# Gate roots moved to GpSimd in eight pieces, third norm's statistics derived from the second's, VectorE side work placed behind the row minimum

## The chip, the cores and the metric

One core of a Trainium2 chip runs the whole program in one launch. The metric is the device time of that core in microseconds (us), the median of several executions; a lower time is better. The engines are TensorE (PE; PEld is its weight load), VectorE (DVE), ScalarE (ACT), GpSimd (POOL) and SyncE (SP, which here only issues DMAs).

## The reference, cut to what matters

The input is 16 sequences of 1024 tokens with 128 features. Each goes through an embedding with six gated convolutions, then a two-map attention, then a feed-forward part with expert weights:

```python
h = tok(x)                                  # embedding, 6 gated convolutions
h = h + attn(layernorm(h))
h = h + ffn(layernorm(h))

# attn, 8 heads of 16 features, L = 1024, windows of 4 rows:
attn1 = softmax(q1 k1 / 4); attn2 = softmax(q2 k2 / 4)
# per window and map: mean, std, max, min of the attention rows
std = jnp.std(r, axis=-1, ddof=1).mean(axis=-1)
alpha = sigmoid(relu(relu(gate_in @ gw1 + gb1) @ gw2 + gb2) @ gw3 + gb3)
out = (alpha * attn1 + (1 - alpha) * attn2) @ v @ Wo

# ffn: normalises its input again
mu = xf.mean(-1); var = xf.var(-1)
normed = (xf - mu) / sqrt(var + 1e-5) * ln_g + ln_b
x_attn = normed @ attn_w.T + attn_b + xf
y = fc2(gelu(fc1(x_attn))); out = gelu(y @ next_w.T + next_b)
```

The ffn normalises what the layernorm before it has already normalised: these are the second and the third norm below. The standard deviation per attention row is a square root of a variance; there are 16 units (2 maps x 8 heads) x 8 row tiles = 128 such columns of 128 rows for a sequence.

## The kernel before, in words

Work on a sequence ("batch") is a fixed pipeline of 128 steps, 16 units j of 8 steps n each; 16 batches follow one another in a loop, with a prologue ahead and a tail behind. In every step

- PE makes a tile of scores (`ps_s`, line 389 by the helper `mm`), adds a tile to the weighted sum (`ps_o`), makes a tile of transposed scores (`ps_t`), and then does the step's side tasks (`ps_w`);
- DVE copies and negates the scores with their maximum (`row_max`, L715, `neg_s`), does the step's side tasks, and then takes the row minimum of the tile before (`row_min`, L723);
- ACT takes the exponential of the transposed scores (`exp_t`, L586), does its side tasks, and then takes the sum of squares of the softmax rows (`squares`, L579, `junk`).

The score buffers are two deep (`ps_s`), so PE can be about two steps ahead of DVE; `ps_t` is single, so PE and ACT alternate on it. Every engine takes its instructions in order.

Side tasks are everything else of the network: the convolutions of the next batch (`conva`, `convg`), projections, the gate and the feed-forward part of the batch before. `plan()` writes them once, before the program is built, into a list for each step (`STEP[n]`); it uses a cost for PE (`COST`), one for POOL (`POOL_COST`, `STEP_WEIGHT`), gaps in steps between tasks (`GAP`), and allowed places within a unit (`SLOTS`). All engines go through the same list in the same order, so a task that waits holds up what stands behind it on its engine.

The tasks that the change touches or that stand near it:

- `snap` (step 16): DVE takes the reciprocal of the softmax sums (L762), POOL then makes the gate's features in `gin` and the two attention outputs (L943 to L959). The variances are left in `gtmp[:, 3, :]`.
- `std` (step 21): two ACT square roots (L610) write the feature columns of `gin`. `win` (step 23) multiplies `gin` on PE, DVE copies the result to `winm` (L764). `hid1`, `hid2`, `logit`, `alpha` follow.
- `msplit` j (two steps ahead of `mrow` j): POOL splits the 8 row maxima of the unit before into three bf16 parts (L866, L914, L916); `mrow` j (first step of unit j) transposes them on DVE (L755), and SP then issues four DMAs of them (L337) and the 12 loads of the next unit (L330). PE needs the rows four steps later.
- `unit` j: DVE takes up a finished unit's output (L731) and POOL two small statistics (L879). For j = 2 DVE waits for POOL's `snap`.
- `convg`: POOL closes a piece of a convolution with four instructions.
- `ln1`, `ln2`, `ln3`: DVE takes mean and variance (`moments`, L735 and L739), POOL normalises (`normalise`, L866, L885, L886, L888). L885 is the power with exponent -0.5 on a 128x8 tile. `ln3` (step 48) is the third norm; it reads `ln2`'s result.

In units 0 and 15 the tasks `qk` (four POOL instructions each) stand ahead of `msplit` 1 and `msplit` 15.

In the tail, after the loop, the same post-processing runs once for the last batch, one task after another, with nothing beside it.

Of the kernel before, what the change touches and what calls it, by code (L numbers as in the profile page):

```python
# [24 lines left out]
P = 128  # L25
L = 1024
# [27 lines left out]
def two(kind):  # L54
    return [(kind, 0), (kind, 1)]
# [5 lines left out]
POST = ([("snap",), ("std",), ("win",), ("hid1",), ("hid2",), ("logit",), ("alpha",)] + two("attT") + two("wo")  # L61
# [5 lines left out]
    "std": ("act",),  # L67
    "win": ("pe", "dve"), "hid1": ("pe", "dve"), "hid2": ("pe", "dve"), "logit": ("pe", "act", "pool"),
    "alpha": ("pe", "dve", "pool"), "attT": ("pe", "act"), "wo": ("pe", "dve"), "ln2": ("dve", "pool"),
    "ln3": ("dve", "pool"), "nT": ("pe", "act"), "attw": ("pe", "act"), "fc1": ("pe", "act"), "gelu1": ("act",),  # L70
# [11 lines left out]
             "ln1": 66, "ln2": 66, "ln3": 66, "gelu2": 24, "vcopy": 15}  # L82
# [3 lines left out]
GAP = {("std",): 5, ("win",): 2, ("hid1",): 2, ("hid2",): 2, ("logit",): 2, ("alpha",): 2, ("attT", 0): 4,  # L86
# [12 lines left out]
def plan():  # L99

    at = {n: [] for n in range(STEPS)}
    for j in range(U):
        at[j * T].append(("mrow", j))
        at[j * T + LAG_V % T - 1].append(("unit", j))
    for n, task in {0: ("gather",), 2: ("vcopy", 0), 3: QK[1][0], 5: QK[1][1], 8: QK[1][2], 10: QK[1][3],
                    14: ("vcopy", 1)}.items():
# [4 lines left out]
    share = cost(BODY_TASKS) / (STEPS - 2 * T)
    behind = 0
    for n in range(STEPS):
        behind = max(behind - STEP_WEIGHT, 0) + sum(POOL_COST.get(t[0], 0) for t in at[n])
        for stage in (post, pre):
            tasks, first = stage
            while tasks and first <= n and n % T in SLOTS.get(tasks[0][0], range(T)):
                task = tasks[0]
                done = cost([t for m in range(n) for t in at[m]])
                on_pe = task[0] in COST  # L120
                if on_pe and (cost(at[n]) or stage is pre and done + COST[task[0]] / 2 > share * (n + 1)):
                    break
                if task[0] in ("conva", "convg") and behind > STEP_WEIGHT:
                    break
                if stage is pre and any(t[0] in ("gelu1", "gelu2", "std") for t in at[n]):
                    break
                at[n].append(tasks.pop(0))
                behind += POOL_COST.get(task[0], 0)
                if task == ("wo", 1):
                    at[n].append(("hcopy",))  # L130
                first = n + (GAP.get(tasks[0], SPREAD.get(tasks[0][0], 1)) if tasks else 0)
            stage[1] = first
    assert not post[0] and not pre[0], (post, pre)
    for j in range(1, U + 1):
# [27 lines left out]
def tower_kernel(nc, ids, table, consts, w_e2h, b_e2h, conv_w, conv_b, w_h2e, b_h2e, wq1, wk1, wq2, wk2, wv, wo,  # L162
# [4 lines left out]
    with ExitStack() as ctx:  # L167
        def sb(name, shape, dt=F32):
            return ctx.enter_context(nc.sbuf_tensor(name, shape, dt))
# [28 lines left out]
        rs_pow = sb("rs_pow", [P, T])  # L198

# [187 lines left out]
        def _(pe):  # L387
# [53 lines left out]
            def task(phase, i, tk):  # L441
# [6 lines left out]
                if kind == "win":  # L448
                    w("act", ("std",))
# [120 lines left out]
        def _(act):  # L570
# [24 lines left out]
            def task(phase, i, tk):  # L595
# [11 lines left out]
                elif kind == "std":  # L607
                    w("pool", ("snap",))
                    for a in range(2):
                        last = nc.scalar.activation(  # L610
                            gin[:, :, :, 4 * a + 1].rearrange("p t h -> p h t"),
                            gtmp[:, 3, U * T // 2 * a:U * T // 2 * (a + 1)].rearrange("p (h t) -> p h t", h=H),
                            ACT.Sqrt)
# [84 lines left out]
        def _(dve):  # L698
# [43 lines left out]
            def task(phase, i, tk):  # L742
# [77 lines left out]
            nc.vector.memset(rs_pow[:, :], -0.5)  # L820
            nc.vector.memset(xc[:, :, 0:1], 0.0)
# [12 lines left out]
            pos.update(loop=True, base=pos["n"], n=0, per=3)  # L834
# [17 lines left out]
        def _(pool):  # L852
# [37 lines left out]
            def task(phase, i, tk):  # L890
# [37 lines left out]
                elif kind == "snap":  # L928
# [22 lines left out]
                    ts(gtmp[:, 3, :], gtmp[:, 1, :], 1.0 / (L - 1), 0.0, ALU.mult, ALU.max)  # L951
# [7 lines left out]
                    last = feature(3, lambda dst, a: tt(dst, of2(0, a), of(recip, a), ALU.mult))  # L959
                elif kind == "logit":  # L960
# [58 lines left out]
            for tk in BODY:  # L1019
                per += {"msplit": 3, "snap": 5, "alpha": 1, "ln2": 3, "ln3": 3, "convg": 3, "ln1": 3, "qk": 3}.get(tk[0], 0)  # L1020
# [62 lines left out]
```

How the kernel before makes its waits and increments, by code:

```python
        def wait_side(eng, phase, i, of, task=None):  # L272
            eng.wait_ge(side_sem[of], side.upto(phase, i, of, task))
# [41 lines left out]
        @block.sync  # L316
# [35 lines left out]
                sp.dma_start(out[i], z[:, :, :]).then_inc(s_out, 16)  # L352
            load_ids(0)
            for dst, src in weight_loads:
                sp.dma_start(dst, src).then_inc(s_load, 16)
            wait_side(sp, "pre", 0, "pool", QK[0][-1])
            load_unit(0)
            with sp.Fori(0, NB // E) as group:
                for e in range(E):
                    i = group * E + e
                    sp.wait_ge(s_emb, i * (16 * T) + 16 * T)
                    settle()
                    load_ids(i + 1)
                    load_expert("body", i, e)
                    for j in range(U):
                        if j:
                            sp.wait_ge(s_st, i * STEPS + T * (j - 3) + T + LAG_T)
                        else:
                            sp.wait_ge(s_exp, i * STEPS + 1)
                        settle()
# [5 lines left out]
                        if ("gelu2",) in sum((STEP[n] for n in range(j * T, j * T + T)), []):  # L378
                            store_out("body", i)
            load_expert("tail", NB, 0)
            store_mrow("tail", NB, 0)
            store_out("tail", NB)
            sp.wait_ge(s_out, 16 * (NB + 2))
# [57 lines left out]
            def task(phase, i, tk):  # L441
# [48 lines left out]
                    _, c, j = tk  # L490
                    if (c, j) == (0, 0):
                        pe.wait_ge(s_exw, i * 64 + 64)
                    w("act", ("attw", c))
```

## Time and profile before

| | us |
|---|---|
| median of 3 runs (5943.18 to 5953.85) | 5952.06 |
| the profiled execution | 5952.66 |
| its span | 5950.7 |
| its granted TensorE clock, mean | 0.947 |

| stretch of the span | us |
|---|---|
| prologue | 0 to 137.5 |
| 2048 steps in 16 batches | 137.5 to 5827.8 |
| tail | 5827.8 to 5950.7 |

The span is that of the instructions; 2 us lie around it. A batch takes 5690.3 / 16 = 355.6 us, a step 2.78 us on average. The sixth batch (1914.4 to 2268.0 us) stands for all: its stretches, and single instructions of it, are read below. A step n of it starts where DVE's L715 starts: step 16 at 1954.1, step 21 at 1966.8, step 24 at 1977.3, step 36 at 2009.1, step 50 at 2051.0, step 80 at 2128.1, step 104 at 2204.8.

### The profile page before, as it was taken

What the parts mean: (1) busy time and instruction counts of PE and PEld (TensorE: products, weight loads), DVE (VectorE), ACT (ScalarE), POOL (GpSimd) and SP (SyncE); (2) the same over time, 40 slices, a digit from 0 to 9 for tenths busy, and PEclk for the clock granted to TensorE, in tenths of its full rate; (3) what the DMA queues carried; (4) which work ended last, traced back from release to release, by engine and by line L of the source; (5) the groups of instructions that cost most, each with busy time, mean ns of one, the idle gap of its engine ahead of it and who ended that gap; (6) DMA issues with size and microseconds to landing.
All of it is one profiled execution on the core that took longest, in us unless ns stands there. A gap on an engine that the chain in (4) does not pass through costs nothing.

```text
span 5950.7 us, 121038 instructions
## 1 busy us (share of the span) xinstructions
PE 5237.1 (88%) x34070; PEld 2513.5 (42%) x34070; DVE 5105.1 (86%) x7715; ACT 5201.0 (87%) x7937; POOL 2445.9 (41%) x4439
## 2 busy tenths in 40 slices
PE   6988989899898988989889898988989899898985
PEld 4443434444343443434344343443435344343443
DVE  2989899898998989899888988989899898989982
ACT  2998989889898999989889898998989889898893
POOL 6525344252433525344352434425353352534422
PEclk8999999999999999999999999999999999999996
DMA  1011010011101001010010101001010110101010
GB/s 38 19 23 27 18 31 20 21 27 24 27 20 29 20 21 27 20 31 19 22 28 22 27 20 28 20 23 27 22 27 20 24 24 21 27 20 30 18 23 10
DMA packets 164934, 140.87 MB, mean 24 GB/s; under 512 B 89197, under 2 KB 108269, under 8 KB 164141
## 3 DMA queue, kind: packets, MB, share of 16 engines
q1 hardware_dynamic: 159100, 124.09, 9.1%
q0 software_dynamic: 4352, 8.92, 0.7%
q8 instruction: 291, 4.77, 0.4%
q14 instruction: 375, 3.06, 0.2%
q10 hardware_dynamic: 816, 0.02, 0.0%
HBM read 21.26 MB, written 8.91 MB: 5 GB/s over the span
## 4 chain that ended last, share of the span: by engine, by line
PE 43%; ACT 24%; issue 15%; DVE 8%; POOL 6%; SPq 1%; ACTq 1%; DMA 1%; POOLq 0%; DVEq 0%
PE ps_w L389 19%; PE ps_t L389 10%; ACT junk L579 10%; ACT exps L586 8%; PE ps_o L389 8%; PE ps_s L389 6%; DVE neg_s L715 4%; DVE rowmin L723 2%; ACT hpre L590 2%; SPq L330 1%; DVE bn L735 1%; POOL part L866 1%; POOL ctmp L998 1%; POOL part L1000 1%; ACT L579 1%
## 5 line engine op out<-in xcount | busy, mean ns | idle before, releaser
L715 DVE TENSOR_SCALAR_CACHE_REDUCE neg_s<-ps_s 128x1024 f32<-128x1024 f32 x2048 | 2492.3, 1217 | 464.2 <-PE ps_s L389 399.0
L579 ACT ACTIVATE junk<-neg_s,negmax 128x1024 bf16<-128x1024 f32 x2048 | 2358.8, 1152 | 227.6 <-DVE neg_s L715 222.6
L723 DVE TENSOR_REDUCE rowmin<-neg_s 128x1 f32<-128x1024 f32 x2049 | 2467.3, 1204 | 0.0
L586 ACT ACTIVATE exps<-ps_t 128x1024 f32<-128x1024 f32 x2060 | 2112.6, 1026 | 171.2 <-PE ps_t L389 166.5
L389 PE MATMUL ps_t<-qst,kst 99*128 99x512 bf16 x4120 | 1300.6, 399 | 441.3 <-ACT exps L586 436.9
L389 PE MATMUL ps_o<-exps,v_cur 128*32 128x256 f32 x16512 | 1365.3, 404 | 133.2 <-DVE o_raw L731 112.2
L389 PE MATMUL ps_s<-kst,qst 96*128 96x512 bf16 x4096 | 1272.0, 392 | 65.3 <-DMA kst<-part 49.2
L389 PE MATMUL ps_w<-xc,cw 128*128 128x256 f32 x4704 | 1199.3, 392 | 1.0
L389 PEld LDWEIGHTS ps_w<-xc,cw 128*128 128x128 f32 x4704 | 922.4, 197 | 229.8 <-ACT chan L590 8.9
L866 POOL TENSOR_SCALAR ctmp<-ug 128x256 f32<-128x256 f32 x408 | 164.7, 404 | 1593.3 <-ACT ug L655 1577.9
L389 PEld LDWEIGHTS ps_t<-qst,kst 99*128 99x128 bf16 x4120 | 237.3, 98 | 1369.3 <-ACT exps L586 771.3
L389 PEld LDWEIGHTS ps_o<-exps,v_cur 128*32 128x32 f32 x16512 | 330.6, 109 | 1061.8 <-issue 691.3
L389 PEld LDWEIGHTS ps_s<-kst,qst 96*128 96x128 bf16 x4096 | 397.4, 101 | 494.5 <-issue 158.9
L579 ACT ACTIVATION_READ_ACCUMULATOR junk<-neg_s,negmax 128x1 f32 x2048 | 412.1, 201 | 0.0
L986 POOL TENSOR_TENSOR ctmp<-ctmp,va 128x256 f32<-128x256 f32 x408 | 297.3, 729 | 34.1
L987 POOL TENSOR_TENSOR ctmp<-ctmp,xc 128x256 f32<-128x256 f32 x408 | 278.5, 683 | 32.0
L866 POOL TENSOR_SCALAR mparts<-negmax 128x8 bf16<-128x8 f32 x256 | 51.8, 202 | 564.8 <-DVE neg_s L715 524.3
L590 ACT ACTIVATE va<-ps_w,cb 128x256 f32<-128x256 f32 x392 | 185.2, 472 | 80.6 <-PE ps_w L389 68.3
L655 ACT ACTIVATE ug<-ps_w,cb_half 128x256 f32<-128x256 f32 x392 | 186.5, 476 | 75.5 <-PE ps_w L389 74.7
L866 POOL TENSOR_SCALAR xc<-ctmp 128x256 f32<-128x256 f32 x408 | 166.5, 408 | 67.7 <-POOL ctmp L987 67.7
L866 POOL TENSOR_SCALAR part<-stage 128x512 bf16<-128x512 f32 x132 | 81.8, 619 | 259.8 <-ACT stage L590 241.2
L715 DVE DVE_READ_ACCUMULATOR neg_s<-ps_s 128x1 f32 x2048 | 168.4, 82 | 0.0
(181 smaller groups left out, 4031.4 us busy)
## 6 DMA issues: line engine op xcount, KB each, us to landing
qst<-part SPq DMA_DIRECT2D x1542, 32.0 KB, 2.0
kst<-part SPq DMA_DIRECT2D x1542, 32.0 KB, 2.0
qst<-mrow SPq DMA_DIRECT2D x1028, 1.5 KB
out_dram<-z SPq DMA_DIRECT2D x17, 512.0 KB, 3.2
fc1s<-in_fc_w SPq DMA_DIRECT2D x17, 256.0 KB
fc2s<-in_fc_w SPq DMA_DIRECT2D x17, 256.0 KB
cw<-in_conv_w SPq DMA_DIRECT2D x1, 2304.0 KB
odif<-in_table,idx POOLq DMA_INDIRECT x136
```

The costliest lines, as they stand in the source:

```text
L330: sp.dma_start(dst[HD * g:HD * g + HD, r, :], part[HD * h:HD * h + HD, a, w, c, :])\
L389: return nc.tensor.matmul(dst, lhs, rhs, start=start, stop=stop, **kw)
L579: nc.scalar.activation(junk[:, n % 2, :], neg_s[:, n % SLOTS_S, :], ACT.Exp, scale=-1.0, bias=negmax[:, r, t:t + 1], accum_out=sumsq[:, r, ...
L586: nc.scalar.activation(exps[:, n % RING, :], ps_t[:, :, :].rearrange("p c q -> p (c q)"), ACT.Exp, scale=0.5).then_inc(s_exp, 1)
L590: return nc.scalar.activation(dst, src, ACT.Identity, **kw)
L655: last = nc.scalar.activation(ug[:, c % 2, :], bank[:, CH:2 * CH], ACT.Tanh, scale=0.5, bias=cb_half[:, 2 * l + 1:2 * l + 2])
L715: nc.vector.tensor_scalar(neg_s[:, n % SLOTS_S, :], ps_s[:, n % 2, :], -1.0, None, ALU.mult, ALU.min, accum_out=negmax[:, r, t:t + 1]).the ...
L723: nc.vector.tensor_reduce(rowmin[:, r, t:t + 1], neg_s[:, m % SLOTS_S, :], axis=AX, op=ALU.max, negate=True).then_inc(s_min, 1)
L735: last = nc.vector.bn_stats(bn[:, t, :], src[:, t, :])
L866: return nc.gpsimd.tensor_scalar(*args)
L986: chain(i, tt(ctmp[:, 1, :], ctmp[:, 0, :], va[:, c % 2, :], ALU.mult))
L987: chain(i, tt(ctmp[:, 2, :], ctmp[:, 1, :], x_in, ALU.add))
```

## The change

Three edits.

1. `std` becomes eight tasks (`STD`) on POOL in place of one on ACT. Each is one `tensor_tensor` with the power operation, exponent 0.5, on 2 heads x 8 row tiles, that is 128x16. The planner gives them cost 20, sees `snap` three steps ahead of the first, and lays one on each of steps 19 to 26; `win` waits for the last one and moves from step 23 to 28. The variance is held above 1e-30.
2. `ln3` leaves DVE: POOL works out the third norm's factor from the second norm's variance and factor (three small instructions, the power, and one multiply of the tile). The mean is taken as zero. POOL's subtract of the mean (L886) goes.
3. On DVE, of a step's tasks only `unit` stays ahead of `row_min`; all others come behind it. `unit` is put first in every list.

By the planner's list the order around the moved pieces is (POOL's part): step 16 `snap`; 18 `convg01`; 19 `std0`; 20 `std1`; 21 `unit2`, `std2`; 22 `std3`, `msplit3`; 23 `std4`, `convg02`; 24 `std5`; 25 `std6`; 26 `std7`; 27 `convg03`; 29 `unit3`; 30 `msplit4`. Before, it was: step 16 `snap`; 18 `convg01`; 20 `convg02`; 21 `unit2`; 22 `msplit3`; 24 `convg03`; 28 `convg10`. DVE's `mrow3` stands in step 24 in both. In the new list `hid1` is in step 30, `hid2` in 32, `wo0` and `wo1` in 43 and 44, `ln2` in 48, `ln3` in 56, `gelu1` in 88 (before: 25, 27, 39, 40, 41, 48, 80), with the convolution pieces between them and again one PE task at most in a step.

```diff
+STD = [("std", k) for k in range(U // 2)]
-POST = ([("snap",), ("std",), ("win",), ...
+POST = ([("snap",)] + STD + [("win",), ...
-    "std": ("act",),
+    "std": ("pool",),
-    "ln3": ("dve", "pool"), ...
+    "ln3": ("pool",), ...
-             "ln1": 66, "ln2": 66, "ln3": 66, "gelu2": 24, "vcopy": 15}
+             "ln1": 66, "ln2": 66, "ln3": 50, "std": 20, "gelu2": 24, "vcopy": 15}
-GAP = {("std",): 5, ...
+GAP = {("std", 0): 3, ...
+    for n in range(STEPS):
+        at[n].sort(key=lambda task: task[0] != "unit")
...
                 if kind == "win":
-                    w("act", ("std",))
+                    w("pool", STD[-1])
...
-                elif kind == "std":
-                    w("pool", ("snap",))
-                    for a in range(2):
-                        last = nc.scalar.activation(... ACT.Sqrt)
...
-                elif kind == "ln3":
-                    w("pool", ("ln2",))
-                    last = moments(i, x2, 1)
...
+            nc.vector.memset(half_pow[:, :, :], 0.5)
...
                         row_max(i, n)
                         for tk in STEP[n]:
-                            task("body", i, tk)
+                            if tk[0] == "unit":
+                                task("body", i, tk)
                         row_min(i, n)
+                        for tk in STEP[n]:
+                            if tk[0] != "unit":
+                                task("body", i, tk)
...
+                elif kind == "std":
+                    a, h = tk[1] // (H // 2), tk[1] % (H // 2) * 2
+                    last = tt(gin[:, :, h:h + 2, 4 * a + 1].rearrange("p t h -> p h t"),
+                              gtmp[:, 3, T * (H * a + h):T * (H * a + h + 2)].rearrange("p (h t) -> p h t", h=2),
+                              half_pow[:, :, :], ALU.pow)
...
                 elif kind == "ln3":
-                    w("dve", tk)
                     w("pe", ("attT", 1))
-                    last = normalise(i, att, x2, 1)
+                    chain(i, tt(rstd[:, 1, :], mv[:, 0, :, 1], rstd[:, 0, :], ALU.mult))
+                    chain(i, tt(rstd[:, 1, :], rstd[:, 1, :], rstd[:, 0, :], ALU.mult))
+                    chain(i, ts(rstd[:, 1, :], rstd[:, 1, :], 1.0, EPS, ALU.mult, ALU.add))
+                    chain(i, tt(rstd[:, 1, :], rstd[:, 1, :], rs_pow[:, :], ALU.pow))
+                    last = tt(att[:, :, :], x2[:, :, :], rstd[:, 1, :].unsqueeze(2).to_broadcast([P, T, P]), ALU.mult)
```

## Rows read from the trace of the kernel before

**Rows 1.** Stretches of the sixth batch: length, busy PE, PEld, DVE, ACT, POOL, granted clock.

```profile
1954.10:1977.30 23.20, 19.89 (x147) 9.60 (x144) 20.17 (x29) 22.51 (x35) 17.04 (x34) 1.00 0.09 20
1977.30:2009.10 31.80, 31.80 (x229) 16.41 (x231) 29.75 (x43) 28.46 (x45) 14.73 (x25) 1.00 0.10 22
```

**Rows 2.** Timeline of DVE, steps 20 and 21: start us, us, engine line op.

```profile
1964.49 1.22 DVE L715 TENSOR_SCALAR_CACHE_REDUCE neg_s<-ps_s 128x1024 f32<-128x1024 f32 x1
...
1965.63 1.22 DVE L723 TENSOR_REDUCE rowmin<-neg_s 128x1 f32<-128x1024 f32 x1
1966.76 1.22 DVE L715 TENSOR_SCALAR_CACHE_REDUCE neg_s<-ps_s 128x1024 f32<-128x1024 f32 x1
```

**Rows 3.** Who waited for whom: us in total, times, longest us.

```profile
DVE winm L764 <- PE ps_w L389: 59.4, 17, 14.0
DVE mrow L755 <- POOL mparts L916: 70.2, 46, 3.8
DVE h_next L794 <- PE ps_w L389: 13.7, 16, 0.9
DVE gtmp L766 <- PE ps_w L389: 12.8, 16, 1.0
DVE h L777 <- PE ps_w L389: 12.3, 16, 0.8
```

**Rows 4.** Timeline of ACT: the two table loads around step 21's square roots.

```profile
1968.82 1.28 ACT L610 ACT_TABLE_LOAD   x1
...
1970.60 1.28 ACT L579 ACT_TABLE_LOAD   x1
```

**Rows 5.** Timeline of DVE: `mrow` in step 8, the third norm's moments, `mrow` in step 120.

```profile
1936.18 0.21 DVE L755 STREAM_TRANSPOSE mrow<-mparts 128x32 bf16<-128x32 bf16 x1 [1.97 <-POOL mparts L916]
...
2045.31 1.62 DVE L735 BATCH_NORM_STATS2 bn<-x 128x6 f32<-128x128 f32 x8
...
2047.59 1.19 DVE L723 TENSOR_REDUCE rowmin<-neg_s 128x1 f32<-128x1024 f32 x1
...
2248.76 0.21 DVE L755 STREAM_TRANSPOSE mrow<-mparts 128x32 bf16<-128x32 bf16 x1 [2.38 <-POOL mparts L916]
```

**Rows 6.** One line's instructions (L885): ns least/median/most, first and last start us.

```profile
L885 POOL TENSOR_TENSOR rstd<-rstd,rs_pow x51: 1636/1647/1676, 100.6 to 5904.5; 128x8 f32<-128x8 f32 x51
```

**Rows 7.** A group of POOL instructions by form: count, busy us, mean ns, idle before.

```profile
L879 POOL TENSOR_TENSOR dif_all<-rowmin,negmax 128x8 f32<-128x8 f32 x258 | 52.3, 203 | 61.0 <-POOL xc L866 39.6 <-POOL part L1000 10.8 <-ACT junk L579 4.2
```

**Rows 8.** Timeline of POOL from `snap` (step 16) to `msplit3` (in step 23).

```profile
1956.77 0.52 POOL L943 TENSOR_TENSOR mean_all<-o_raw,recip 128x128 f32<-128x128 f32 x1 [1.40 <-DVE recip L762]
...
1967.50 0.59 POOL L959 TENSOR_TENSOR gin<-gtmp,recip 128x64 f32<-128x64 f32 x2
1968.33 0.40 POOL L866 TENSOR_SCALAR ctmp<-ug 128x256 f32<-128x256 f32 x1 [0.24 <-POOL gin L959]
...
1970.42 0.40 POOL L866 TENSOR_SCALAR xc<-ctmp 128x256 f32<-128x256 f32 x1 [0.16 <-POOL ctmp L987]
...
1973.84 0.20 POOL L879 TENSOR_TENSOR dif_all<-rowmin,negmax 128x8 f32<-128x8 f32 x1 [0.30 <-POOL xc L866]
...
1975.55 0.20 POOL L916 TENSOR_TENSOR mparts<-mrest,mparts 128x8 bf16<-128x8 f32 x1
```

**Rows 9.** Timeline of PE behind ACT's Gelu block (step 82).

```profile
2139.30 1.03 PE L389 MATMUL ps_t<-qst,kst 99*128 99x512 bf16 x2 [5.76 <-ACT exps L586]
```

**Rows 10.** The stretch around it: length, busy PE, PEld, DVE, ACT, POOL, granted clock.

```profile
2138.00:2144.00 6.00, 4.70 (x14) 2.66 (x18) 0.21 (x1) 4.64 (x9) 2.18 (x4) 0.50 0.14 30
```

**Rows 11.** Timeline of the tail: the gate's start and the third norm.

```profile
5869.23 0.60 POOL L959 TENSOR_TENSOR gin<-gtmp,recip 128x64 f32<-128x64 f32 x2
...
5870.47 1.89 PE L389 MATMUL ps_w<-cst,gin 128*64 128x32 f32 x16 [13.70 <-ACT gin L610]
...
5901.71 1.65 DVE L735 BATCH_NORM_STATS2 bn<-x 128x6 f32<-128x128 f32 x8 [6.08 <-POOL x L888]
...
5908.22 1.90 POOL L888 TENSOR_TENSOR odif<-odif,rstd 128x1024 f32<-128x1024 f32 x1
```

More of the change, by code:

```diff
@@ L60 @@
 PRE = [("gather",)] + two("embT") + two("e2h") + CONV + two("h2e") + [("ln1",)] + two("xnT") + QK[0] + two("v")
-POST = ([("snap",), ("std",), ("win",), ("hid1",), ("hid2",), ("logit",), ("alpha",)] + two("attT") + two("wo")
+STD = [("std", k) for k in range(U // 2)]
+POST = ([("snap",)] + STD + [("win",), ("hid1",), ("hid2",), ("logit",), ("alpha",)] + two("attT") + two("wo")
         + [("ln2",), ("ln3",)] + two("nT") + [("attw", c) for c in range(NC)]
@@ L66 @@
     "msplit": ("pool",), "mrow": ("dve",), "unit": ("dve", "pool"), "vcopy": ("pool",), "hcopy": ("pool",), "snap": ("dve", "pool", "act"),
-    "std": ("act",),
+    "std": ("pool",),
     "win": ("pe", "dve"), "hid1": ("pe", "dve"), "hid2": ("pe", "dve"), "logit": ("pe", "act", "pool"),
     "alpha": ("pe", "dve", "pool"), "attT": ("pe", "act"), "wo": ("pe", "dve"), "ln2": ("dve", "pool"),
-    "ln3": ("dve", "pool"), "nT": ("pe", "act"), "attw": ("pe", "act"), "fc1": ("pe", "act"), "gelu1": ("act",),
+    "ln3": ("pool",), "nT": ("pe", "act"), "attw": ("pe", "act"), "fc1": ("pe", "act"), "gelu1": ("act",),
     "fc2": ("pe", "act"), "next": ("pe", "dve"), "gelu2": ("act", "pool"), "gather": (), "embT": ("pe", "act"),
@@ L81 @@
 POOL_COST = {"msplit": 8, "unit": 5, "qk": 35, "convg": 23, "gather": 85, "snap": 80, "alpha": 46, "hcopy": 20,
-             "ln1": 66, "ln2": 66, "ln3": 66, "gelu2": 24, "vcopy": 15}
+             "ln1": 66, "ln2": 66, "ln3": 50, "std": 20, "gelu2": 24, "vcopy": 15}
 STEP_WEIGHT = 27
-GAP = {("std",): 5, ("win",): 2, ("hid1",): 2, ("hid2",): 2, ("logit",): 2, ("alpha",): 2, ("attT", 0): 4,
+GAP = {("std", 0): 3, ("win",): 2, ("hid1",): 2, ("hid2",): 2, ("logit",): 2, ("alpha",): 2, ("attT", 0): 4,
        ("wo", 0): 2, ("ln3",): 5, ("nT", 0): 6, ("attw", 0): 2, ("gelu1",): 1, ("fc2", 0): 4, ("next", 0): 2,
@@ L124, in plan @@
                     break
-                if stage is pre and any(t[0] in ("gelu1", "gelu2", "std") for t in at[n]):
+                if stage is pre and any(t[0] in ("gelu1", "gelu2") for t in at[n]):
                     break
@@ L198, in tower_kernel @@
         rs_pow = sb("rs_pow", [P, T])
+        half_pow = sb("half_pow", [P, 2, T])
         part = sb("part", [P, 2, 2, 3, L], BF16)
@@ L606, in task @@
                                                 ACT.Exp, scale=0.5)
-                elif kind == "std":
-                    w("pool", ("snap",))
-                    for a in range(2):
[L610 to L613, printed above, removed]
                 elif kind == "logit":
@@ L833, in _ @@
                 task("pre", 0, tk)
-            pos.update(loop=True, base=pos["n"], n=0, per=3)
+            pos.update(loop=True, base=pos["n"], n=0, per=2)
             with dve.Fori(0, NB // E) as group:
@@ L950, in task @@
                     chain(i, tt(gtmp[:, 1, :], gtmp[:, 2, :], gtmp[:, 1, :], ALU.subtract))
-                    ts(gtmp[:, 3, :], gtmp[:, 1, :], 1.0 / (L - 1), 0.0, ALU.mult, ALU.max)
+                    ts(gtmp[:, 3, :], gtmp[:, 1, :], 1.0 / (L - 1), 1e-30, ALU.mult, ALU.max)
                     heads = lambda t: t[:, :, :].rearrange("p t (h d) -> p t h d", h=H)
@@ L1019, in _ @@
             for tk in BODY:
-                per += {"msplit": 3, "snap": 5, "alpha": 1, "ln2": 3, "ln3": 3, "convg": 3, "ln1": 3, "qk": 3}.get(tk[0], 0)
+                per += {"msplit": 3, "snap": 5, "alpha": 1, "ln2": 3, "ln3": 4, "convg": 3, "ln1": 3, "qk": 3}.get(tk[0], 0)
             pos.update(loop=True, base=pos["n"], n=0, per=per)
```

## The prediction

> **What bounds the kernel now.** I read first the busy time by stretch of one batch, then the timeline of DVE, then the table of waits, then POOL's timeline where the new work goes. A batch is 128 steps in 355.6 us. In the stretches no engine is idle by much except POOL: in steps 16 to 23 ACT is busy 22.51 of 23.20 us, in steps 24 to 35 PE is busy all 31.80 us and DVE 29.75 [rows 1]. So three engines stand close to each other, and the step is set by whichever is late. The floor is DVE's: the negating copy and the row minimum follow each other without a gap, a step starts 2.27 us after the one before, and the minimum alone takes 1.13 us of that [rows 2]. 128 such steps are 290 us; the other 65 us of a batch are side work and waits, and that is what a change of this sort can move. POOL's busy share says the least here: in steps 16 to 23 it is busy 17.04 of 23.20 us [rows 1], and this is where the change lays its eight powers.
>
> **What is removed, per batch.** The third norm's moments hold DVE from 2045.31 to 2047.59: 2.3 us [rows 5], beside nothing that replaces them. The wait of `win`: DVE waits 59.4 us in 17 cases; without the tail's 14.0 it is 45.4 / 16 = 2.8 us a batch [rows 3]. Its cause is on ACT: two table loads and two roots lie between 1968.82 and 1971.88, 3.06 us [rows 4], PE's transposed scores come late by that and `win` behind them. With ACT's part gone this cause is gone. The order on DVE: a task that waits for PE now waits while the minimum runs, which covers up to 1.13 us. The three waits of `h_next`, `hid1` and `h` (13.7 + 12.8 + 12.3) / 16 = 2.4 us a batch, each under 1.0 us [rows 3], go whole. Of the waits for `msplit` (70.2 / 16 = 4.4 us a batch) nearly all is the two of 1.97 and 2.38 us [rows 3, 5]; POOL stays late there, so each shrinks by one minimum, 2.3 us together. In steps 24 to 35 DVE is idle 31.80 - 29.75 = 2.05 us; less the 0.8 us of `hid1`, 1.25 us are PE's debt after the stall [rows 1, 3]; it goes with its cause. Sum: 2.3 + 2.8 + 2.4 + 2.3 + 1.25 = 11.05 us.
>
> One thing goes the other way already here. `snap`'s reciprocal now comes behind step 16's minimum, so POOL's `snap` starts 1.13 us later; it lasts from 1956.77 to 1968.09, 11.3 us [rows 8], and DVE's `unit2` in step 21 waits for its end. That leaves some 10 us of gain. What hides POOL's three extra small instructions of `ln3`: its result has six steps to the next task, and it loses the subtract.
>
> The load of the ACT tables is 1.28 us each way in the rows, and the next activation follows it at once [rows 4]. The Trainium skill ("ScalarE: Activation LUTs", What ACT_TABLE_LOAD costs) puts a drain of about 1.38 us on each switch beside the load. By it, the two switches would be worth 2.8 us more a batch and the result 44 us less; the rows show no such gap, so I go by them.
>
> **What is added: eight powers of 128x16 on POOL.** No row shows one. The nearest is the norms' power on 128x8, 1.65 us, and it hardly varies [rows 6]; a plain two-operand instruction on the same 128x8 takes 0.20 us [rows 7]. Lower bound for 16 columns: nothing grows, 1.65 us. Upper: all but the plain cost grows with the columns, 0.20 + 2 x 1.45 = 3.1 us. I take the upper: 1.45 us above a plain instruction that reads, writes and starts in the same way is work on the values, and the values double. A gain is excluded, as twice the columns can't be cheaper. Each piece waits for POOL's own instruction before it, which costs 0.24 us where a row shows such a pair [rows 8]: 3.34 us a piece (1.89 at the lower bound).
>
> So a piece a step is more than a step. In POOL's queue from `snap`'s end on stand: `convg01` 0.24 + 2.49 = 2.73 us (1968.33 to 1970.82), `std0`, `std1`, `unit2`, `std2`, `std3`, `msplit3`; `unit2` and `msplit3` take 1.91 us from 1973.84 to 1975.75 and a gap of 0.30 [rows 8]. `msplit3` ends 2.73 + 4 x 3.34 + 2.2 = 18.3 us after `snap`. DVE comes to `mrow3`, behind step 24's minimum, 1.13 + 3 x 2.27 us and a take-up of a unit after `snap`'s end, about 8.4 us [rows 2]. It waits 9.9 us. Behind `mrow3` stand the next row maximum, and so PE's scores and all else.
>
> Then come `std4`, `convg02`, `std5` to `std7`: they end at 18.3 + 4 x 3.34 + 2.73 = 34.4 us, and `win` on PE takes about 1 us more. DVE, at four steps of 2.27 us from 18.5 us on and with step 28's minimum done, is ready for `winm` at 27.8: a second wait of 7.6 us. In it PE stands at `win` with scores and transposed scores queued behind. Then PE is in debt as it is now after a `win` stall, 1.25 us. Lastly the clock: where PE idled 5.76 us behind ACT's Gelu block, the granted clock of the next 6 us is 0.50 (1.2 GHz) and a pair of transposed scores takes 1.03 us [rows 9, 10], while the stretches ahead have 1.00 [rows 1]. After two idle spells of that length I allow 1 us (none to 3). Sum added: 9.9 + 7.6 + 1.25 + 1.0 = 19.8 us a batch.
>
> Net: 19.8 - 10 = 9.8 us a batch, 157 us in 16.
>
> **The tail** has no cover. `snap`'s end to `win` is 5870.47 - 5869.83 = 0.64 us now [rows 11]; eight pieces are 26.7 us. The third norm takes 5901.71 to 5910.12, 8.4 us [rows 11]; without moments and subtract, but with two products, a scaling, the power and the last multiply, it is about 4.7 us by the rows of its parts [rows 6, 7, 11]. Tail: +26.7 - 0.6 - 3.7 = +22 us.
>
> **Sum.** The profiled execution's 5952.66 us + 157 + 22 = 6132; it lies 0.6 us above the median shown, so 6130 us.
>
> **Rivals.**
>
> *The power is mostly a fixed cost* (a piece is 1.65 to 2.0 us). For it: all 51 powers agree within 40 ns, and a program may spend that on setting up; no second size is in the trace [rows 6]. Against it: it would have to be seven times a plain instruction's whole time. Then `msplit3` ends at 12.5 us, `mrow3` waits 4.1 us, `winm` 1.8, the debt is 1.25: 7.15 against 10, -2.85 x 16 = -46, tail +11: 5918 us. It decides below 2.1 us a piece; there stalls and gains are equal and the change is faster.
>
> *Between* (2.4 us): waits of 7.1 and 4.8 us, 13.65 with debt and half the clock term, +3.65 x 16 + 17 = +75: 6028 us.
>
> *The gains on DVE don't arrive*: PE and ACT are so near the bound [rows 1] that half of the 10 us only uncovers them, with the power at 3.1 us: 5 x 16 = 80 more, 6210 us.
>
> *POOL hides the powers wholly*: a piece would have to cost like a plain instruction, 0.2 us; then no queue forms and the 10 us stay, tail -1: 5790 us. The 1.65 us of half a piece speak against it [rows 6].
>
> [...] The power's row is eight times what it gives, so I keep one chance in a hundred.
>
> **How the numbers follow.** Chances: the forecast 0.57, gains that don't arrive 0.06, between 0.13, fixed cost 0.23, hidden 0.01. For 8 in 10 the range leaves out the hidden case, the lower edge of the fixed one and the upper edge of the worst: 5915 to 6200 us. Within the forecast's own case, a piece of 2.8 to 3.2 us and 3 us a batch of error on the gains give 6050 to 6190. A measurement here tells about 0.2% (12 us) from no change. Faster: most of the fixed case and a part of the one between, 0.26. Within 0.2%: 0.07. Slower: 0.67.
>
> **What would show it.** In the profile after: the mean of the power on 128x16 (3.1, or near 1.7); DVE waiting for `msplit` at 9 to 10 us in step 24 and for `win` at 7 to 8 us in step 28; no table load for roots and two loads fewer a batch; the waits of `h`, `h_next` and `hid1` near nothing; no moments on the third norm; a longer gap before `win` in the tail. The prediction is wrong if the piece is under 2.1 us; it is wrong in its mechanism if POOL has the pieces done before DVE and PE come to `mrow3` and `win`, or if the time rises somewhere else, as at the unit loads that now start one minimum later.

## The result and the profile after

The changed kernel takes 6169.75 us (median of 4, 6161.59 to 6175.42) beside 5949.48 for the kernel before on the same chip: ratio 1.037, interval 1.0352 to 1.0388. The profiled execution's span is 6166.6 us, 215.9 more than before. A batch takes 368.2 us instead of 355.7, which makes 200 us in 16 batches; the tail behind the last row maximum takes 139.8 instead of 124.1, which makes 15.7 more.

First the page after: the engines' busy time (share of the span, instructions), the shares of the chain that ended last (a q marks an engine's queue; "issue" is time in which an engine waited for nothing that the profile shows), and the group of the new powers (count, busy us, mean ns, idle before).

```profile
PE 5312.3 (86%) x34070; PEld 2555.7 (41%) x34070; DVE 5074.2 (82%) x7444; ACT 5159.5 (84%) x7869; POOL 2816.8 (46%) x4592
...
PE 40%; ACT 20%; POOL 17%; issue 15%; DVE 5%; SPq 2%; POOLq 1%; ACTq 1%; DMA 1%; DVEq 0%
...
L961 POOL TENSOR_TENSOR gin<-gtmp,half_pow 128x16 f32<-128x16 f32 x136 | 397.5, 2923 | 10.9
```

A piece is 2.92 us; the norms' power on 128x8 was 1.65 [rows 6]. So there is a fixed part and one that grows: if the exponent and the layout of the output don't matter, which no run tests, the two points give 0.16 us a column and some 0.37 us besides. POOL is busy for less than half of the span and yet holds 17% of the chain, where before it held 6%. Which place that is, the table of waits says (us in total, times, longest).

```profile
DVE neg_s L712 <- PE ps_s L393: 518.3, 579, 20.0
...
DVE winm L761 <- PE ps_w L393: 138.3, 17, 37.5
DVE mrow L752 <- POOL mparts L915: 136.8, 45, 7.0
...
PE ps_w L393 <- POOL gin L961: 124.4, 17, 37.3
```

`mrow` waits 136.8 us where it waited 70.2, and `winm` 138.3 where it waited 59.4 [rows 3]; of the 138.3, 37.5 are the tail's. The waits of `h_next`, `hid1` and `h` for `ps_w` that stood in the same table [rows 3] are gone, and so are the roots' two table loads a batch on ACT. The first row has grown; before, it was this:

```profile
DVE neg_s L715 <- PE ps_s L389: 399.0, 442, 20.0
```

The sixth batch shows both waits. POOL's timeline from `snap`'s end on (start us, us, engine line op; instructions alike that follow each other are one row):

```profile
2030.96 0.60 POOL L958 TENSOR_TENSOR gin<-gtmp,recip 128x64 f32<-128x64 f32 x2
2031.81 0.40 POOL L865 TENSOR_SCALAR ctmp<-ug 128x256 f32<-128x256 f32 x1 [0.24 <-POOL gin L958]
...
2034.38 5.95 POOL L961 TENSOR_TENSOR gin<-gtmp,half_pow 128x16 f32<-128x16 f32 x2
...
2041.47 5.92 POOL L961 TENSOR_TENSOR gin<-gtmp,half_pow 128x16 f32<-128x16 f32 x2
...
2048.63 0.20 POOL L915 TENSOR_TENSOR mparts<-mrest,mparts 128x8 bf16<-128x8 f32 x1
2048.91 2.93 POOL L961 TENSOR_TENSOR gin<-gtmp,half_pow 128x16 f32<-128x16 f32 x1
...
2054.66 8.91 POOL L961 TENSOR_TENSOR gin<-gtmp,half_pow 128x16 f32<-128x16 f32 x3
```

And DVE's, of which only the rows with a wait stand here (in brackets the idle time before the instruction and what ended it):

```profile
2031.69 0.45 DVE L728 STREAM_TRANSPOSE o_raw<-ps_o 128x256 f32<-128x256 f32 x1 [1.43 <-POOL gin L958]
...
2036.78 1.23 DVE L712 TENSOR_SCALAR_CACHE_REDUCE neg_s<-ps_s 128x1024 f32<-128x1024 f32 x1 [1.26 <-PE ps_s L393]
...
2048.95 0.21 DVE L752 STREAM_TRANSPOSE mrow<-mparts 128x32 bf16<-128x32 bf16 x1 [6.90 <-POOL mparts L915]
...
2065.57 0.42 DVE L761 COPY winm<-ps_w 64x256 f32<-64x256 f32 x1 [6.46 <-PE ps_w L393]
```

`msplit3` stands behind four powers, and DVE waits 6.90 us for it in step 24. `win` stands behind all eight, and DVE waits 6.46 us for it in step 28. PE, in the same places:

```profile
2032.20 0.96 PE L393 MATMUL ps_o<-exps,v_cur 128*32 128x256 f32 x8 [3.19 <-DVE o_raw L728]
...
2050.37 1.03 PE L393 MATMUL ps_s<-kst,qst 96*128 96x512 bf16 x2 [4.57 <-DVE neg_s L712]
...
2063.62 1.91 PE L393 MATMUL ps_w<-cst,gin 128*64 128x32 f32 x16 [5.80 <-POOL gin L961]
```

Within each of the three idle spells, or just behind it, the granted clock falls to 0.50 (1.2 GHz) for some microseconds. Two of these stretches and a third, in step 101, on which more below (length, busy PE, PEld, DVE, ACT, POOL, granted clock):

```profile
2049.44:2056.27 6.83, 5.76 (x19) 2.79 (x20) 6.55 (x9) 4.64 (x8) 6.19 (x6) 0.50 0.11 23
2059.68:2069.92 10.24, 6.30 (x32) 3.93 (x33) 3.11 (x5) 1.41 (x3) 6.38 (x8) 0.50 0.03 6
2271.31:2278.14 6.83, 6.20 (x20) 3.12 (x21) 2.60 (x4) 4.66 (x8) 2.67 (x6) 0.50 0.27 78
```

All stretches at 0.50 together are 43.3 us a batch, where before had 31.1.

The tail, on POOL: eight powers on the path, and a third norm of 4.5 us (6121.99 to 6126.52) where it took 8.4 [rows 11].

```profile
6067.72 23.88 POOL L961 TENSOR_TENSOR gin<-gtmp,half_pow 128x16 f32<-128x16 f32 x8
...
6121.99 0.20 POOL L978 TENSOR_TENSOR rstd<-mv,rstd 128x8 f32<-128x8 f32 x1
...
6124.63 1.89 POOL L982 TENSOR_TENSOR odif<-x,rstd 128x1024 f32<-128x1024 f32 x1
```

### The profile page after: what moved, and what is told of

Same layout as the page of the kernel before. It is cut to its first block, busy times and chain, and to the rows that moved or that the text cites. A ratio compares the mean times of both kernels' runs of the same rounds, so it can differ in the third digit from the quotient of the medians.

```text
span 6166.6 us, 120899 instructions
## 1 busy us (share of the span) xinstructions
PE 5312.3 (86%) x34070; PEld 2555.7 (41%) x34070; DVE 5074.2 (82%) x7444; ACT 5159.5 (84%) x7869; POOL 2816.8 (46%) x4592
## 3 DMA queue, kind: packets, MB, share of 16 engines
q14 instruction: 375, 3.07, 0.2%
HBM read 21.26 MB, written 8.91 MB: 5 GB/s over the span
## 4 chain that ended last, share of the span: by engine, by line
PE 40%; ACT 20%; POOL 17%; issue 15%; DVE 5%; SPq 2%; POOLq 1%; ACTq 1%; DMA 1%; DVEq 0%
PE ps_w L393 18%; PE ps_t L393 9%; ACT junk L583 8%; PE ps_o L393 7%; POOL gin L961 6%; PE ps_s L393 6%; ACT exps L590 6%; DVE neg_s L712 2%; ACT hpre L594 2%; SPq L334 2%; POOL part L865 1%; POOL ctmp L1005 1%; POOL part L1007 1%; POOL ctmp L993 1%; POOL ctmp L994 1%
## 5 line engine op out<-in xcount | busy, mean ns | idle before, releaser
L393 PE MATMUL ps_w<-xc,cw 128*128 128x256 f32 x4704 | 1245.4, 403 | 1.4
L393 PEld LDWEIGHTS ps_w<-xc,cw 128*128 128x128 f32 x4704 | 953.0, 204 | 254.9 <-issue 23.9
L961 POOL TENSOR_TENSOR gin<-gtmp,half_pow 128x16 f32<-128x16 f32 x136 | 397.5, 2923 | 10.9
```

The costliest lines, as they stand in the source:

```text
L393: return nc.tensor.matmul(dst, lhs, rhs, start=start, stop=stop, **kw)
L961: last = tt(gin[:, :, h:h + 2, 4 * a + 1].rearrange("p t h -> p h t"), gtmp[:, 3, T * (H * a + h):T * (H * a + h + 2)].rearrange("p (h t) ...
```

## The experiments

To compare runs, the steps of each trace (from one row maximum to the next) are averaged over the 16 batches and added up by stretch. In us per batch; the columns behind "after" are the experiments in the order below, "plain" standing for products in place of powers. The last lines are the tail of the profiled execution, from the start of the last row maximum on, and the measured ratio to the kernel before:

```
steps     before  after  plain roots   old    old   conv   only  spread spread spread spread snap
                               on ACT  order  ln3   later  order        tail   ACT    plain  first
0-20        53.1   52.5   52.6   52.9   53.4   52.7   53.2   52.6   52.2   52.2   52.2   52.4   52.2
21-23       10.7   11.0   11.1   10.0    9.2   11.4   10.7   10.3   10.4   10.7   10.5   10.9    8.8
24-27       12.9   16.7    9.4   11.2   18.2   16.1   16.9   11.2    9.8    9.7    9.8    9.6    9.9
28-29        4.9   14.3    5.5    5.3   13.7   14.2   14.3    5.3    4.9    4.9    4.9    5.0    4.9
30-35       15.6   16.6   16.6   16.2   16.6   16.6   16.6   16.2   14.8   14.6   13.7   13.7   14.9
36-63       76.0   74.1   74.1   74.6   74.7   74.5   74.1   75.3   75.5   75.7   80.2   75.0   76.0
64-119     159.4  160.7  160.7  158.8  160.8  159.3  160.7  159.0  156.0  156.1  156.2  155.7  155.8
120-127     23.2   22.4   22.4   22.3   23.0   22.4   22.3   22.2   21.9   21.9   21.9   21.9   22.0
batch      355.7  368.2  352.4  351.4  369.6  367.1  368.7  352.1  345.6  345.8  349.4  344.3  344.5
tail       124.1  139.8  116.8  118.8  144.6  147.0  142.4  117.1  142.4  113.5  116.3  119.9  116.8
ratio        1    1.037  .9913  .9892  1.0404 1.0357 1.0396 .9909  .9775  .9730  .9826  .9688  .9704
```

The tail's lines differ by more than its code does: `snap` starts there between 26.1 and 32.5 us after the last row maximum, and the runs "after", "old order", "conv later" and "spread", whose tails are alike, have 139.8, 144.6, 142.4 and 142.4 us. A difference of a few us in that line alone shows nothing.

The theory at the start was that of the prediction: the powers' 3 us each in POOL's queue hold `msplit3` and `win`, and all the rest of the change brings some 10 us a batch. The rivals were that the loss lies elsewhere, and that the 10 us never arrive.

**The powers' price alone.** A product is short, 0.226 us as the rows below show; all else is the changed kernel.

```diff
-                              half_pow[:, :, :], ALU.pow)
+                              half_pow[:, :, :], ALU.mult)
```

> The changed kernel with the power of the eight pieces replaced by a plain product with 0.5 (the roots are left out): the same instructions in the same places, only short. Theory (POOL's queue of eight long powers is the loss): the waits of mrow3 in step 24 and of win in step 28 go, steps 21 to 35 fall from 58.6 us to about 41 us, 17.7 us a batch, and the tail by 22 us: 6170 - 283 - 22 = 5865 us. Rival (the moved side work and the new task list cost as much as they bring, the power only adds): 5940 us or more. Rival (the loss is not in POOL's queue): stays above 6080 us.

Measured: 5892.87 us, ratio 0.9913 (0.9897 to 0.993): nearest the theory. The group of the product, and the waits in this run:

```profile
L961 POOL TENSOR_TENSOR gin<-gtmp,half_pow 128x16 f32<-128x16 f32 x136 | 30.7, 226 | 10.9
```

```profile
DVE neg_s L712 <- PE ps_s L393: 463.4, 533, 20.0
...
DVE mrow L752 <- POOL mparts L915: 36.1, 27, 2.4
...
PE ps_w L393 <- POOL gin L961: 15.7, 1, 15.7
```

The powers, thirteen times the product's time, are worth 368.2 - 352.4 = 15.85 us a batch and 23 us of tail, of which 3 are an earlier start of `snap`; they are the whole loss and more. The wait for `msplit` falls by (136.8 - 36.1) / 16 = 6.3 us a batch, that for `win` by as much. But against the kernel before only 355.7 - 352.4 = 3.4 us a batch are left, not 10. The first row says where the rest is: DVE's row maximum waits 463.4 us for PE's scores, 64 more than before. The Trainium skill ("GPSIMD Engine Reference", 3.1 Elementwise — side-by-side cycle accounting) puts a two-operand instruction at about 2.6 cycles an element, measured on an add, and has no figure for a power; here the same instruction on the same tiles takes 0.226 us as a product and 2.923 as a power, so a figure for plain operations can't stand for the power.

**Roots back on ACT, the other two edits kept.**

```diff
-    "std": ("pool",),
+    "std": ("act",),
...
+                elif kind == "std":
+                    w("pool", ("snap",))
+                    for a in range(2):
+                        last = nc.scalar.activation(
...
+                            ACT.Sqrt)
```

> Only the first edit undone: the roots are two ACT instructions again, in step 21; third norm and DVE's order as in the changed kernel. Theory (the other two edits are gains that arrive): against before, 2.3 us a batch from the third norm's moments, 2.4 from the waits of h_next, hid1 and h, 2.25 from the two long mrow waits, 1.1 from a minimum in the wait of win, less 1.0 for the later snap: 7.1 us x 16 and 4 in the tail, 5832 us. Rival (PE and ACT are so near the bound that half is only uncovered): about 5890 us. Rival (the two edits do nothing): 5950 us.

Measured: 5879.88 us, ratio 0.9892 (0.9875 to 0.9908). It is nearest the rival in which half of the gains only uncover other engines: 4.4 us a batch and 5 of tail. With the roots back the planner's list is that of the kernel before again, but for convolution pieces between steps 49 and 92, each of which stands earlier than there.

**The old order on DVE, the other two edits kept.**

```diff
-                            if tk[0] == "unit":
-                                task("body", i, tk)
+                            task("body", i, tk)
                         row_min(i, n)
```

> Only the third edit undone: DVE's side work ahead of the row minimum again, powers on POOL. Theory: where DVE waits for POOL or PE a minimum no longer runs in the wait: 1.1 us each in steps 8, 24, 28 and 120, 2.4 us for h_next, hid1 and h, less 1.2 us for snap's earlier start: 5.7 us a batch, 6260 us. Rival (the order brings nothing): within 15 us of 6170.

Measured: 6186.42 us, ratio 1.0404 (1.0387 to 1.0422): much nearer the rival than the theory. The order is worth 1.35 us a batch here. Steps 24 to 27 lose 1.5 us more without it, but steps 21 to 23 take 1.8 less: there `snap` starts earlier.

**The old third norm, the other two edits kept.**

```diff
+                elif kind == "ln3":
+                    w("pool", ("ln2",))
+                    last = moments(i, x2, 1)
```

> Only the second edit undone: the third norm's moments on DVE again, in the new task list. Theory (DVE's 2.3 us come back whole): 2.3 x 16 + 4 in the tail, 6210 us. Rival (PE is behind there and uses the time to catch up, so that most of the 2.3 us is covered): 6170 to 6185 us.

Measured: 6157.51 us, ratio 1.0357 (1.034 to 1.0375). The second case holds, and beyond it: the kernel with the extra 2.3 us of DVE work is not slower. Step 56 takes 2.26 us more and steps 57 to 61 take 1.9 less: PE and ACT catch up while DVE has the moments. But the moments aren't all that differs: the planner leaves step 57 free behind them, and the convolution pieces up to step 96 stand later than in the changed kernel. How much of the catching up is that isn't shown. The rest comes from step 101 (5.31 us, in the changed kernel 6.52). Here is PE behind ACT's second Gelu block, in the changed kernel and then in this one:

```profile
2271.94 1.03 PE L393 MATMUL ps_t<-qst,kst 99*128 99x512 bf16 x2 [2.85 <-ACT exps L590]
2272.76 2.77 PE L393 MATMUL ps_w<-xc,cw 128*128 128x256 f32 x6
```

```profile
2265.90 0.61 PE L393 MATMUL ps_t<-qst,kst 99*128 99x512 bf16 x2 [2.85 <-ACT exps L590]
2266.35 1.48 PE L393 MATMUL ps_w<-xc,cw 128*128 128x256 f32 x6
```

The idle time is the same to the hundredth; in the first the clock is 0.50 and the convolution takes 2.77 us, in the second this stretch has 1.00:

```profile
2264.70:2271.50 6.80, 5.60 (x36) 3.12 (x36) 3.96 (x6) 6.75 (x13) 2.96 (x8) 1.00 0.27 78
```

It isn't one batch's chance: the clock is 0.50 in step 101 in all 16 batches of the changed kernel and in 2 of 16 here. So the half clock after a stall of this size is not to be had from the stall alone. What PE had done before differs a little, as convolution `conva(5,2)` stands in step 96 here and in step 91 there. Whether that decides isn't shown by these runs.

**The convolution moved out of that step.**

```diff
+    at[101].remove(("conva", 5, 3))
+    at[102][at[102].index(("convg", 5, 3))] = ("conva", 5, 3)
+    at[103][at[103].index(("h2e", 0))] = ("convg", 5, 3)
+    at[104].append(("h2e", 0))
```

> The changed kernel with all its edits; only the list of tasks is altered by hand behind gelu2: the convolution conva(5,3) goes from step 101 to 102, convg(5,3) from 102 to 103, the first h2e from 103 to 104, so that the step in which the clock falls to 0.50 after ACT's Gelu block holds no side task of PE. The whole computation is kept. Theory (the dear part of the half clock is what PE has to do in it: six matmuls of 0.63 us where they take 0.38): step 101 falls from 6.5 to about 3.8 us, the steps 102 to 104 give some of it back, and about 2 us a batch are gained: 6130 to 6140 us where the changed kernel has 6165 to 6175. Rival (the low clock and the work are only moved to step 102): within 8 us of the changed kernel, 6160 to 6180.

Measured: 6178.73 us, ratio 1.0396 (1.0378 to 1.0413): the rival. Step 101 falls to 4.36 us, and step 102 rises from 3.08 to 4.99; the convolution meets the low clock one step on:

```profile
2279.84 2.71 PE L397 MATMUL ps_w<-xc,cw 128*128 128x256 f32 x6
```

**The order alone, on the kernel before.** The edits to the roots and to the third norm are undone.

> The kernel before with only the third edit: DVE does its side work but the unit tasks behind the step's minimum. Roots on ACT, the third norm with its own moments on DVE. The whole computation is kept. The run with roots on ACT and the other two edits took 5880 us. Theory (the third norm from the second's statistics brings next to nothing in the batches, 0.5 us each, and some 4 us in the tail, since PE makes up the lost time in the steps behind): 5892, 5885 to 5900 us. Rival (it brings its whole 2.3 us a batch when POOL has no queue, and the order brings the rest): 5915 to 5925.

Measured: 5888.73 us, ratio 0.9909 (0.9892 to 0.9925): the theory. The order brings 355.7 - 352.1 = 3.6 us a batch, the third norm on top of it (the run with roots on ACT) 0.8. There step 48 falls from 4.67 to 2.41 us, and steps 50 to 53 give 1.84 of it back. The list of this run is that of the kernel before to the letter, so the 3.6 are the order's; the 0.8 hold the moved convolution pieces too.

DVE's waits in the run with the order alone, and one row of the kernel before:

```profile
DVE neg_s L719 <- PE ps_s L393: 446.1, 562, 20.0
...
DVE mrow L759 <- POOL mparts L925: 32.9, 27, 2.6
...
DVE o_raw L735 <- POOL gin L968: 22.3, 16, 1.4
...
DVE winm L768 <- PE ps_w L393: 16.8, 7, 14.1
```

```profile
DVE o_raw L731 <- POOL gin L959: 3.8, 16, 0.2
```

Less the tail's 14.1 us, DVE waits 0.2 us a batch for `win`, where it waited 2.8, and the roots are still on ACT. So the order is enough to end this wait. What comes in its place is the first row: 446.1 us where before had 399.0, which is 2.9 a batch.

**The same powers, spread.** The planner is told what a power costs and to leave two steps from one to the next: they stand in steps 23, 25 to 37, the first of them behind `msplit3`, and `win` in step 39.

```diff
-             "ln3": 50, "std": 20,
+             "ln3": 50, "std": 31,
...
-GAP = {("std", 0): 3,
+GAP = {("std", 0): 7, **{("std", k): 2 for k in range(1, U // 2)},
```

> The changed kernel with the same eight powers on POOL, but the planner told their measured cost (31 for 20) and a gap of two steps from each to the next: they come to stand in steps 23, 25, to 37, win in step 39, and all that follows some ten steps later (gelu2 in 107). The whole computation is kept. Theory (it is where the pieces stand in POOL's queue, ahead of msplit3 and win, not POOL's 23 us of work a batch): DVE's wait for msplit in step 24 and PE's for win go, the batches come near the 352 us that they take with plain products in place of powers, and the tail keeps its 22 us: 5890 to 5950. Rival (POOL's work itself, or its use of what DVE also uses, slows the others): 6080 or more.

Measured: 5809.15 us, ratio 0.9775 (0.9758 to 0.9791): the place decides, not POOL's work; and it is 81 us below the range that I gave. The powers are as long as before (2.926 us), POOL is as busy (2818.1 us against 2816.8), and the waits shrink: that of `mrow` to less than before's 70.2 us, that of `winm` to the tail's:

```profile
DVE neg_s L712 <- PE ps_s L393: 235.9, 455, 20.0
...
DVE mrow L752 <- POOL mparts L915: 63.0, 74, 2.8
PE ps_w L393 <- POOL gin L961: 46.9, 17, 37.3
DVE winm L761 <- PE ps_w L393: 40.5, 17, 37.5
```

In POOL's timeline `msplit3` now ends just ahead of the first power:

```profile
1930.30 0.20 POOL L915 TENSOR_TENSOR mparts<-mrest,mparts 128x8 bf16<-128x8 f32 x1
1930.58 5.95 POOL L961 TENSOR_TENSOR gin<-gtmp,half_pow 128x16 f32<-128x16 f32 x2
```

The batch is 6.8 us shorter even than with plain products in the changed kernel's list. So the new list brings something of its own: stretches at 0.50 are 20.9 us a batch, where the run with products had 28.4 and the changed kernel 43.3. The next three runs take this apart.

**The tail's roots on ACT**, the batches as in the spread version.

```diff
-TAIL = [("mrow", 0), ("unit", 0), ("unit", 1)] + POST
+TAIL = [("mrow", 0), ("unit", 0), ("unit", 1), ("snap",), ("root",)] + POST[1 + len(STD):]
```

> The spread powers, but in the tail behind the last batch the roots are taken by ACT in two instructions, as in the kernel before; the batches are those of the spread version. The whole computation is kept. Theory (in the tail nothing hides eight powers of 2.9 us): the tail falls from 142 us to about 120, so 5788 us, 5780 to 5798. Rival (something else in the tail ends as late): 5803 to 5812, no change.

Measured: 5786.72 us, ratio 0.973 (0.9717 to 0.9744); as expected. The tail falls from 142.4 to 113.5 us, of which 5 are an earlier start of `snap`.

**The spread list to the letter, roots on ACT** in step 37.

```diff
+STEP = [[("std",) if t == LAST else t for t in s if t[0] != "std" or t == LAST] for s in plan().values()]
```

> The spread version's list of steps to the letter, but the roots are taken by ACT in two instructions in step 37, where the last power stood; POOL has no powers. The whole computation is kept. It tells what the roots' place on ACT costs from what the new list itself brings: the spread version takes 5809 us and the changed kernel with roots on ACT in step 25 took 5880. Theory (most of the gain is the list's, which has fewer half-clock spells of PE; ACT's block of two roots with its table loads costs 1.5 to 3 us a batch, and the tail is some 22 us shorter): 5810 to 5835. Rival (the gain comes from ACT being rid of the roots): 5860 to 5880.

Measured: 5845.13 us, ratio 0.9826 (0.9811 to 0.9841): between the two cases. (The earlier run with roots on ACT has them in step 21, not 25.) ACT, then PE and the stretch behind the block, around step 38:

```profile
1981.11 1.01 ACT L593 ACTIVATE exps<-ps_t 128x1024 f32<-128x1024 f32 x1
1982.14 1.28 ACT L617 ACT_TABLE_LOAD   x1
1983.43 0.46 ACT L617 ACTIVATE gin<-gtmp 128x64 f32<-128x64 f32 x2
1983.91 1.28 ACT L586 ACT_TABLE_LOAD   x1
1985.21 1.15 ACT L586 ACTIVATE junk<-neg_s,negmax 128x1024 bf16<-128x1024 f32 x1
```

```profile
1987.41 0.86 PE L396 MATMUL ps_t<-qst,kst 99*128 99x512 bf16 x2 [2.33 <-ACT exps L593]
...
1992.86 2.26 PE L396 MATMUL ps_w<-xc,cw 128*128 128x256 f32 x6
```

```profile
1987.63:1994.46 6.83, 6.83 (x34) 3.92 (x33) 2.90 (x5) 4.28 (x7) 3.06 (x8) 0.50 0.00 0
```

ACT's block is 3.07 us (1982.14 to 1985.21); PE idles 2.33 us behind it and then works at 0.50, in all 16 batches alike. Each table load is followed by the next activation within 0.02 us, and the activation ahead of the block ends 0.02 us before it. The drain of about 1.38 us that the Trainium skill ("ScalarE: Activation LUTs", What ACT_TABLE_LOAD costs) puts beside each load doesn't show here either.

**The spread list with products in place of powers.** The edit is that of the first experiment.

> The spread version with a product in place of each of the eight powers: the roots are left out, the features in their place are half the variance. Theory (spread over fifteen steps the powers cost the batches nothing, and only the tail has them on its path): 5809 less some 23 us of tail, 5780 to 5793. Rival (POOL's 21 us of extra work a batch still delay it somewhere): each us a batch is 16 us more, 5770 or less.

Measured: 5764.52 us, ratio 0.9688 (0.9673 to 0.9703): the rival. Spread, the eight powers still cost 345.6 - 344.3 = 1.3 us a batch, besides the tail; in the changed kernel's list they cost 15.85. And with the list held, ACT's roots cost 349.4 - 344.3 = 5.1 us a batch, more than the block itself. Steps 39 and 40 take all of it; there the clock is 0.50 in every batch with the roots on ACT, and in none with products.

**`snap`'s reciprocal ahead of the minimum again**, on the version with spread powers and the tail's roots on ACT.

```diff
-                            if tk[0] == "unit":
+                            if tk[0] in ("unit", "snap"):
                                 task("body", i, tk)
```

> The spread powers with the tail's roots on ACT, and DVE takes snap's reciprocal ahead of step 16's minimum again, as in the kernel before; all other side work but the collection stays behind the minimum. The whole computation is kept. In the version without this edit (5787 us) the collection in step 21 waits 1.4 us for the end of POOL's snap, PE idles 3.2 us behind it, the clock falls to 0.50 and step 22's convolution takes its matmuls at that clock: the steps 21 and 22 take 4.12 and 4.30 us. Theory (snap's later start is the cause of both, the wait and the half clock): they fall to about 2.9 and 2.7, 2.8 us a batch, 5742 us, 5735 to 5755. Rival (only the 1.1 us of the later start come back, PE is late there anyway): 5765 to 5775. Rival 2 (the reciprocal ahead of the minimum costs as much as it brings): 5782 to 5792.

Measured: 5770.29 us, ratio 0.9704 (0.9691 to 0.9718): the first rival. Step 21 falls from 4.12 to 2.85 us, step 22 only from 4.30 to 3.64. PE's convolution there waits for ACT's `va`, and ACT for POOL, in the version without this edit and in this one:

```profile
1925.00 0.47 ACT L594 ACTIVATE va<-ps_w,cb 128x256 f32<-128x256 f32 x1 [3.43 <-POOL xc L872]
```

```profile
1916.51 0.47 ACT L594 ACTIVATE va<-ps_w,cb 128x256 f32<-128x256 f32 x1 [2.08 <-POOL xc L872]
```

That `xc` is the end of `convg01`, the next task behind `snap` in POOL's queue: another short task behind a long one. The half clock and PE's 3.2 us of idle time that the expectation names are the changed kernel's; in the spread list the clock is 0.50 in steps 21 and 22 in 6 of 16 batches, and with this edit in none. This is the quickest version that computes all: 3.0% below the kernel before, and by the two ratios 6.4% below the changed one (0.9704 / 1.037).

## Why the prediction was right, and where its terms were not

The forecast was 6130 us, the result 6169.75. The mechanism is shown: with products for powers the loss is gone, and with the same powers spread, the first of them behind `msplit3`, it is gone too. The terms, predicted and measured in us a batch (measured: waits as the difference to the run with products; debt and clock as what these leave of 15.85; the removed work by the runs named):

```
                                        predicted   measured
a piece with its gap                       3.34       2.97
mrow's wait for msplit3                    9.9        6.3
winm's wait for win                        7.6        6.3
PE's debt and the clock                    2.25       3.3
added                                     19.8       15.85
order: waits 2.4 + 2.3, snap -1.1          3.6        3.6   (order alone)
third norm's moments                       2.3        0.8   (on top of the order, with its list)
roots off ACT: win 2.8, debt 1.25          4.05      -1.0   (products against roots on ACT)
removed                                   10          3.4
net                                        9.8       12.5
tail                                      22         15.7
```

**The piece** came from the upper bound, 3.1 us, and is 2.92; three in a row take 8.91. The norms' power takes eight times a plain instruction's 0.20 us on the same tile [rows 6, 7], the new one thirteen times a product's; so the case in which POOL hides the powers wholly was rightly given next to no chance. The gap of 0.24 us that I took from a convolution's row [rows 8] isn't paid between powers. From `snap`'s end (2031.57) to `msplit3`'s (2048.83) it is 17.3 us, 18.3 by the sum.

**The waits were too long by DVE's arrival.** I let DVE run at 2.27 us a step up to `mrow3` and come there 8.4 us after `snap`'s end. It came after 10.5 (2042.05). In step 22 the scores came 1.26 us late and in step 23 another 0.55 was lost. The cause is the later `snap`: I priced it at 1.1 us, DVE's wait of 1.43 us is that price, but behind it PE idled 3.19 us on the collection, the clock fell, and step 22's convolution ran at it. Of the predicted 9.9 us the quicker pieces took 1.0 and this 2.1.

**The clock** I allowed 1 us, after two spells. There are three, and the 16 matmuls of `win`, which I put at about 1 us, take 1.91. The first of the three, behind the later `snap`, stands in the run with products too, so it isn't in the 15.85 us; it lowers the gains. Debt and clock together were only 1 us short.

**The gains were the worst term**: 10 predicted, 3.4 there, less even than in the rival "gains don't arrive", which kept half. The step that failed is the counting of a removed wait or a removed piece of work at its own length. For the order the total came out to the tenth, but not by its parts, and that is luck: the waits of `h_next`, `hid1` and `h` went whole (2.4) and those of `mrow` shrank by 2.3, as I had it, but the wait for `win` went as well (2.7), which I had put down to the roots; against that DVE waited 1.2 us more for `snap` and 2.9 more for PE's scores. For the moments 1.8 of 2.3 us come back a few steps later, where PE and ACT had used the time to catch up; the planner's list, which differs there, has an unknown share in it. For the roots, the wait for `win` was already gone by the order, and the new list costs more than it brings: up to step 63 the run with products is 0.9 us a batch shorter than the run with roots on ACT, but steps 64 to 119 take 160.7 us where that has 158.8. Some of this stands behind the second Gelu block, at half clock: the block's step and the four behind it take 17.2 us (99 to 103), in the run with roots on ACT 16.0 (91 to 95). In the spread list, and from step 37, the same removal is worth 5.1, near the 4.05, but by another way than the one I gave: there it is the clock and PE's idle time behind ACT's block. I had not looked at what the planner makes of the steps behind.

**The tail**: the powers take 23.9 us, 26.7 predicted, and the third norm 4.5, 4.7 predicted. Of the 6.3 us that the tail came out below the sum the pieces explain 2.8. Another 2.5 are the start of `snap`, 29.4 us after the last row maximum where before had 31.9, which differs as much between runs whose tails are alike (32.0 in the run with the old order). The remaining 1 us stays open.

The two errors, 4 us too much added and 6.6 too much removed, went against each other. The total is nearer than its parts: with gains of 3.4 and the waits as I had them the sum would have been 6237 us, outside the range. That the time came out so near to 6130 us is in part luck.

## What to carry to other kernels

An engine that is idle half of the time can still hold the whole kernel: ask which short task stands behind the new work in its queue, and who waits for that one. The same eight instructions cost 15.85 us a batch ahead of two such tasks and 1.3 behind the one and spread. Price a removed wait by what the other engines do with the time, and where a planner lays out the work, lay out its new list before counting any gain: here the list alone was worth up to 8.1 us a batch (products in either list, 352.4 and 344.3).

## What was not expected of the hardware

- A power on POOL takes 1.65 us for 8 columns and 2.92 for 16, where a product takes 0.20 and 0.226: at these two sizes most of its time grows with the columns.
- A stall of PE costs more than itself: behind 3.07 us of ACT's roots the batch lost 5.1 us; PE idled 2.33 us, and the matmuls of the next 6.83 us ran at 1.2 GHz (at this clock a convolution takes 2.26 to 2.77 us instead of 1.46). Moving the convolution by one step only moved the cost.
- The same idle time of 2.85 us behind the same block ended in a granted clock of 0.50 in all 16 batches of one kernel, and of 1.00 in 14 of 16 in another. What decides stays open.
